# Segment sums of a graph layer: one semaphore step for two products, and bounds of sums at even numbers

## The reference, cut to what matters

```python
xn = _layernorm(x)
# for each of 16 relations a matrix Wf and a matrix Wb
m_forward  = segment_sum((einsum('ni,rio->rno', xn, Wf)[etypes, src] + bias) * norm_f, dst, n)
m_backward = segment_sum((einsum('ni,rio->rno', xn, Wb)[etypes, dst] + bias) * norm_b, src, n)
x = x + (2 * xn @ loop_weight + self_bias + m_forward + m_backward) + mixer(xn)
x = x + expert_ffn(_layernorm(x))      # 8 experts, the best 2 of each token
```

## Time and profile before

| | us |
|---|---|
| median of three runs | 2249.82 |
| lowest and highest run | 2246.55, 2253.24 |
| the profiled execution | 2245.63 |
| its span, first to last instruction | 2243.7 |
| TensorE busy | 2015.8 |
| VectorE busy | 1138.3 |
| GpSimd busy | 1027.6 |
| ScalarE busy | 605.0 |

### The profile page before, as it was taken

One profiled execution on the slowest core, in us unless ns is written; L12 is line 12 of the kernel. 1 busy time (PEld: TensorE's weight loads), 2 busy tenths in 40 slices (PEclk: granted clock), 3 DMA queues, 4 the chain that ended last, 5 costly groups with the idle time before them and its releaser, 6 DMA issues.

```text
span 2243.7 us, 26429 instructions
## 1 busy us (share of the span) xinstructions
PE 2015.8 (90%) x8235; PEld 1379.3 (61%) x8235; DVE 1138.3 (51%) x2452; ACT 605.0 (27%) x1262; POOL 1027.6 (46%) x1014
## 2 busy tenths in 40 slices
PE   7999999889999999898878788898989669999997
PEld 3456544355555555454545555677777668888897
DVE  4999950256666564433566656544455841111121
ACT  2333333211221221111422221222222552222242
POOL 0000000366666666666566666666665113333332
PEclk9999999999999999999899999999999579999999
DMA  7432335455555555556644444332334384444473
GB/s 276 158 136 95 134 155 229 159 158 177 179 178 179 178 168 182 178 181 165 184 144 138 146 138 122 90 90 87 87 90 80 128 288 112 125 116 120 128 194 67
DMA packets 136486, 333.20 MB, mean 149 GB/s; under 512 B 25344, under 2 KB 65952, under 8 KB 135072
## 3 DMA queue, kind: packets, MB, share of 16 engines
q1 hardware_dynamic: 80064, 199.64, 24.5%
q0 software_dynamic: 52992, 130.09, 23.1%
q10 hardware_dynamic: 3296, 1.80, 0.3%
HBM read 202.71 MB, written 128.71 MB: 148 GB/s over the span
## 4 chain that ended last, share of the span: by engine, by line
PE 80%; issue 6%; another core or an unknown queue 5%; DVE 4%; ACT 3%; DMA 2%; DVEq 0%; POOL 0%; SPq 0%; ACTq 0%; POOLq 0%
PE bank L679 29%; PE bank L748 15%; PE bank L1947 9%; PE bank L1958 8%; PE bank L1867 4%; PE bank L1876 4%; PE bank L586 3%; DVE arena L773 1%; PE bank L1777 1%; PE bank L1805 1%; DMA table_fwd<-arena 1%; PE bank L1765 1%; PE bank L1844 1%; PE bank L1916 1%
## 5 line engine op out<-in xcount | busy, mean ns | idle before, releaser
L679 PE MATMUL bank<-arena,work 128*128 128x512 f32 x1600 | 741.9, 600 | 14.2 <-ACT arena L672 9.0
L773 DVE TENSOR_TENSOR arena<-arena,bank 128x257 f32 x880 | 370.8, 421 | 529.7 <-PE bank L748 284.1
L748 PE MATMUL bank<-arena 128*128 128x257 f32 x1760 | 499.2, 396 | 71.1 <-DVE arena L773 37.6
L725 POOL DMA_INDIRECT arena<-table_bwd,arena x440 | 428.3, 974 | 237.4 <-issue 99.0
L725 POOL DMA_INDIRECT arena<-table_fwd,arena x440 | 437.2, 994 | 212.8 <-issue 99.8
L679 PEld LDWEIGHTS bank<-arena,work 128*128 128x128 f32 x1600 | 301.3, 192 | 296.5 <-issue 270.8
L672 ACT ACTIVATE arena<-bank 128x512 f32<-128x512 f32 x400 | 238.5, 598 | 777.4 <-PE bank L679 551.7
L748 PEld LDWEIGHTS bank<-arena 128*128 128x128 f32 x1760 | 327.7, 197 | 194.8 <-issue 153.7
L1017 POOL DMA_INDIRECT out<-xn,work x56 | 89.4, 1597 | 250.9 <-DVE xn L192 181.3
L1947 PE MATMUL bank<-xn,arena 128*128 128x256 f32 (+1 forms) x1120 | 203.0, 340 | 0.0
L734 DVE TENSOR_TENSOR arena<-cst,arena 128x512 f32<-128x512 f32 x220 | 151.2, 689 | 102.0 <-PE bank L679 102.0
(11 more groups left out here) (315 smaller groups left out, 1563.8 us busy)
## 6 DMA issues: line engine op xcount, KB each, us to landing
table_fwd<-arena SPq DMA_DIRECT2D x100, 512.0 KB
table_bwd<-arena SPq DMA_DIRECT2D x100, 512.0 KB
arena<-in_W SPq DMA_DIRECT2D x35, 1024.0 KB
arena<-in_W SPq DMA_DIRECT2D x2, 4096.0 KB, 14.3
arena<-table_fwd,arena POOLq DMA_INDIRECT x440
arena<-table_bwd,arena POOLq DMA_INDIRECT x440
work<-x_transposed SPq DMA_DIRECT2D x50, 128.0 KB
mix_rows<-arena SPq DMA_DIRECT2D x25, 256.0 KB
```

The lines of the kernel that those rows point to most:

```text
L679: last = pe.matmul(ps[4 + s % 2][:, :], xT[t % 2][:, k * P:(k + 1) * P], ar(W_off[d] + k * 4096 + c * 512, 512), start=(k == 0), stop=(k = ...
L725: e.indirect_dma_start(msg[b][:, 0:C], None, table[d], bass.IndirectOffsetOnAxis(ap=idx[d][:, n % TE:n % TE + 1], axis=0)).then_inc(s_ga[b ...
L748: pe.matmul(ps[sum_bank(n)][:, 0:W], oh[b], msg[b], start=True, stop=True).then_inc(s_sm, 1)
L773: vec.tensor_tensor(to, to, ps[sum_bank(n)][:, 0:W], ALU.add).then_inc(s_ac, 1)
```

## The change

A product of a list raises `s_sm` only when its number is odd, so once for two products. An add of list n waits for step n // 2 + 1, so the add of an even list waits for the odd one's product as well; a gather waits for (n - 16) // 2 + 1. Adds still raise `s_ac` one by one, and a product still waits for its bank's own add.

So that VectorE never waits for a product which TensorE makes only after something that needs VectorE, all bounds between stages become even. `forward_upto`, `rows_upto`, `keys_upto` and `mlp_step` are rounded down to even numbers, and `M1E`, `KME` and `M2E` move down by one. A stage's turns thus hold 2 or 4 sums in place of 2 or 3 (projections), 4 or 6 in place of mostly 5 (rows), 0 or 2 in place of 1 or 2 (keys and MLP steps). The last sum on three banks is number 287 and no longer 288. The number of products, adds and gathers is the same.

```diff
         def gather(e, n):
             d, b = n // TE, n % RING
-            G.wait(s_sm, n - RING + 1)
+            G.wait(s_sm, (n - RING) // 2 + 1 if n >= RING else 0)
...
-            pe.matmul(ps[sum_bank(n)][:, 0:W], oh[b], msg[b], start=True, stop=True).then_inc(s_sm, 1)
+            product = pe.matmul(ps[sum_bank(n)][:, 0:W], oh[b], msg[b], start=True, stop=True)
+            if n % 2 == 1:
+                product.then_inc(s_sm, 1)
...
-                e.wait_ge(s_sm, n + 1)
+                e.wait_ge(s_sm, n // 2 + 1)
...
         def forward_upto(s):
-            return min(TE - LEFT, max(0, (s - 2) * (TE - LEFT) // (SLOTS - 4)))
+            return min(TE - LEFT, max(0, (s - 2) * (TE - LEFT) // (SLOTS - 4) // 2 * 2))
...
-        M1E, KME, M2E, MCE, M3E, M4E = (TE + n for n in (111, 117, 147, 156, 206, 212))
+        M1E, KME, M2E, MCE, M3E, M4E = (TE + n for n in (110, 116, 146, 156, 206, 212))
...
-            return TE - LEFT + (LEFT + 111) * t // NT
+            return TE - LEFT + (LEFT + 111) * t // NT // 2 * 2
...
-            return KME + 6 * t // 5
+            return KME + 6 * t // 5 // 2 * 2
...
-            return M4E + (2 * TE - M4E) * min(k, steps) // steps
+            return M4E + (2 * TE - M4E) * min(k, steps) // steps // 2 * 2
...
-                add_sums(e, rows_upto(NT - 1) + 2, M1E + 1)
+                add_sums(e, rows_upto(NT - 1) + 2, M1E + 2)
...
-                sums(e, M1E, M1E + 1)
+                sums(e, M1E, M1E + 2)
...
-                sums(e, M2E, M2E + 3)
+                sums(e, M2E, M2E + 4)
...
-                sums(e, M3E, M3E + 3)
+                sums(e, M3E, M3E + 4)
```

More of the change, by code:

```diff
@@ L1252, in _ @@
                 q_rest(NT - 1)
-                add_sums(e, M1E + 1, KME)
+                add_sums(e, M1E + 2, KME)
                 V.mark(vec.memset(KXT, 0.0))
@@ L1796, in _ @@
                 last.then_inc(s_xp, 1)
-                sums(e, M1E + 1, KME)
+                sums(e, M1E + 2, KME)
                 e.wait_ge(s_kqc, NT)
@@ L1814, in _ @@
                 last.then_inc(s_xp, 1)
-                sums(e, M2E + 3, M2E + 6)
+                sums(e, M2E + 4, M2E + 6)
                 e.wait_ge(s_xa, ZBT)
@@ L1882, in _ @@
                 z2_transpose(0)
-                sums(e, M3E + 3, M4E)
+                sums(e, M3E + 4, M4E)
                 for i in range(TURNS):
```

## The result

The changed kernel takes 2,254.6 us (median of 15 runs, 2,247.0 to 2,261.0), the kernel before 2,248.5 in the same set (15 runs): 1.0027 times as long, interval 1.0014 to 1.0039, so 6 us more. Forecast were 16 us less. The time lies in the stated range of 2,192 to 2,267 us, but the change makes the kernel slower and not faster. The profiled execution took 2,251.14 us.

A forecast was written before the change was run, and what follows sets the result against it. TensorE, busy 90% of the span, was taken to lose time among the gathers to its late reports. Terms -28 + 5 + 6 + 1 = -16 us gave 2,234 us, range 2,192 to 2,267.

The forecast's parts named there:

- What bounds the kernel: Among the gathers, TensorE's late reports hold up other engines and return as waits; at most 148 us of idle time.
- 440 reports fewer: Among the gathers, fewer reports pile up at 1.43 us each, so waits shrink and gathers quicken: -28 us, bounds -37 to 0.
- first rival: Lateness comes from the gathers, not the number of reports; only costs remain, +12 us (2,262 us), at most +21; chance 0.28.
- The costs: Added waits in projections, turns over the rows, keys and MLP: +5, +6 and +1 us; +12 at their middle, +21 at top.
- Four sums on three banks: Projections, 10 slots: the fourth product waits for the first add, 0.25 to 0.7 us each; 3 to 7 us, taken +5.
- Turns over the rows: In turns of six sums, the fifth and sixth wait for the first and second add: 0 to 12 us, taken +6.
- Keys and MLP: Keys' turns and MLP steps hold 0 or 2 sums in place of 1 or 2: +1 us for both.
- The price of 0 for an increment in TensorE's own stream: TensorE's matmuls of sums: raising a semaphore costs nothing, spacing stays 0.217 us; the skill's estimate would be 11.6 us.
- The gathers wait for pairs: GpSimd's even gathers wait for one sum more, 15 buffers serving where 16 did; they lead by over ten sums: 0.
- The signs that I named: Gathers towards 1.43 us, GpSimd's sum waits below 160.5, gelu waits below 14.8, long ScalarE waits rare, projections ending earlier.
- the signs of the costs: More wait for VectorE's adds in the turns over the rows than 12.7 us, and new small ones before 870 us.
- The projections' end: The end of the projections, at 1,066 us before, was to come about 10 us earlier.

The follow-up runs named there:

- even bounds alone: Kernel before with only the bounds between stages made even, one report and one wait per sum: 2,249.6 us, 1.0017; with plain DMAs 2,052.6 us.
- with reports on time: Plain DMAs of 128 neighbouring rows in place of the indirect gathers, under both kernels: kernel before 2,048.6 us, changed kernel 2,060.1 us.
- plain changed kernel: Changed kernel with plain DMAs of neighbouring rows in place of the indirect gathers: 2,060.1 us in one set of runs, 2,059.3 us in a later one.
- pair wait alone: Plain DMAs, even bounds, one report per sum, even adds waiting for the odd product, beside the changed kernel with plain DMAs: 2,060.3 us against 2,059.3.
- fifth set: Last group of runs: kernel before 2,078.5 us, with three memsets ahead of each gather 2,257.5; with plain DMAs, changed 2,059.3, even adds' wait only 2,060.3.
- first set: Earliest group of runs: kernel before 2,245.8 us; variants were even bounds, gathers waiting for adds, a memset before each gather, plain DMAs (2,051.7 us).

## Why the prediction was wrong

**What bounds the kernel: right, and incomplete.** Reports of TensorE that come late among the gathers do hold the other engines up and come back to it as waits. With the indirect gathers replaced by plain DMAs, 194 us go: 132 of idle time of TensorE (227.9 to 95.8 us) and 62 of busy time. The prediction set the most that could be had at the 148 us that TensorE idles, and left out the busy time. It is in good part clock: TensorE is busy for 130.6 us at its lower level before and for 56.0 with plain DMAs, and half of that difference, 37 us, is my estimate for it.

**The step that failed** is "440 reports fewer": that the reports pile up because one takes 1.43 us to get through. The 1.43 us of the earlier trace rows were two late starts, not the capacity of anything. Priced at -28 us, it measured nothing: the gathers' pace is 1.476 us as before, their idle time 446 us for 450, the late share 47% for 51% (49% with the even bounds alone). The first rival is what happened: "the lateness does not come from the number of reports but from the gathers". It had 0.28. I had counted the gathers' constant pace for it, and that row could not tell the two apart: by the counts of the prediction TensorE raised 1.09 reports a microsecond in the projections ((424 + 200 + 78) / 644), 1.07 in the turns over the rows ((121 + 75) / 184), 1.16 in the keys' stage ((99 + 25 + 50) / 150) and 1.10 in the MLP ((223 + 142) / 331), so a queue of a fixed rate would have given a constant pace as well.

The recorded numbers spoke against the step before any run. The reports of the prediction's own count, 1,450 at 1.43 us each, need 2,074 us, and all of them got through in 1,311.

**The costs: their sum came out, their parts only in part.** Forecast were +12 us (range to 21); with reports on time the change costs 11.5. *Four sums on three banks*, +5 (3 to 7): right in place and mechanism, 3.3 us in ten waits ahead of the fourth sums. *Turns over the rows*, +6: TensorE idles 4 us more there, but not where the prediction put it. The fifth and the sixth sum hardly wait for adds (0.5 us in all); the self-loop product waits longer for VectorE. *Keys and MLP*, +1: between -0.7 and +0.8 us each. Some 4 us of the 11.5 are found in no stage, so that the sum fits so well is luck in part. By parts of the code, the even bounds take 4.0 and the even adds' wait for the odd product 7.5.

In the kernel with late reports +6 are left (3 to 9). Where engines start 1 to 2 us late anyway, a wait of 0.43 us more for the other product is often already over; that the difference of 5 us comes from this is argued from the timelines, and the two intervals nearly touch. In the two profiled executions the longer time stands in TensorE's busy time at the lower clock and not in its idle time. The prediction's sum had no term for the clock, and what ties the clock to the change is not shown.

**The price of 0 for an increment in TensorE's own stream: right.** Where the four matmuls of two sums follow each other directly, the third starts 216 ns after the second, as the median of the traces, when the second raises the semaphore (kernel before, 157 places) and when it doesn't (changed kernel, 349). The plain changed kernel and the one with the pair wait alone differ by 440 steps and take 2,059.3 and 2,060.3 us. The Trainium skill (TensorE: Matmul & The Clock Gate, The cost: per-tile semaphore tail) gives 26.3 ns to each increment, which would be 11.6 us here as an estimate; this pair does not agree. That section of the Trainium skill fits a tail behind a group of packed tiles, and here it is a stream of full-size matmuls.

**The gathers wait for pairs, 0:** nothing contradicts it. The same pair shows only this wait and the fewer steps together.

**The signs that I named.** "GpSimd's wait for sums falls well below 160.5" came true (99.8) and meant nothing, since the time moved to "remote" and "issue". The gelu's wait shrank to 11.4 us and meant as little, with "issue" up by 6.2. ScalarE's pauses of over 3 us ahead of a projection's copy did not get rare (50 among the gathers, 52 before). The pace and the late starts, which I named as what would refute the step, did so. Of the signs of the costs, new waits for adds before 870 us came (14.9 us for 6.3). The other did not: in the turns over the rows they fell from 12.7 us to 4.3. The projections' end came 1 us earlier in this profile (1,063.8 for 1,065.0), not 10.

**What stays open:** what in an indirect gather holds TensorE's steps back, whether scattered rows or the recording have a part in it, where between 1.42 and 1.60 us it ends, where the last 4 of the 11.5 us lie, and why the kernel before took 2,078.5 us in the fifth set. The records give that chip the same number as the first set's, so a difference between chips doesn't explain it by itself.

## What to carry to other kernels

Where an engine starts late and the one it waits for has long ended, count how late its releases come (start of the waiting instruction less end of the released one) in stages with different work, before you blame the number of releases; and exchange the one neighbour that all late stretches share, here the indirect gather for a plain DMA, before any fine edit. Judge a wait by all the idle time ahead of a group, not by one row of it: 60 us can leave a row and turn up under another name. Cut each trace at its own stages: a kernel that is 194 us faster passes another stage in the same window of time. Before you trust a rate read from two neighbouring events, multiply it by the number of events and compare with the time that they took. A step for two products costs the consumer one product's time each second time, which needs cover, and gives nothing unless the steps themselves cost something.

## What the runs showed of the hardware

- While GpSimd starts an indirect gather each 1.25 us, about half of TensorE's recorded semaphore steps take effect over 0.1 us after the matmul's modelled end, 0.8 us on average (kernel before, changed, even bounds). VectorE's and ScalarE's recorded steps come on time, 11 and 9 ns behind, but only 55% of them are in these records. With plain DMAs of the same size, or with indirect ones 1.60 us apart (one run), TensorE's steps come 14 ns behind.
- In these runs it didn't depend on the rows of a gather (64 or 128), on what GpSimd itself waits for, or on the number of steps that TensorE raises.
- Plain DMAs in place of the indirect gathers were worth 194 us of 2,246 where reports were late. The same kernel took 2,246, 2,230 and 2,078.5 us on different occasions, and its forms with plain DMAs 2,049 to 2,060 on each occasion that had them.
- A matmul that raises a semaphore does not delay the next one: 216 ns from start to start with and without.
